# Turning the next chunk's sampling weights between the two samplings of a slot

## The chip, the cores and the metric

The kernel runs on one core of one Trainium2 chip. The metric is the device time of one execution in microseconds (us). The engines are TensorE (PE: matmuls and transposes), VectorE (DVE), ScalarE (ACT), GpSimd (POOL) and SyncE (SP, which only issues DMAs here). PE writes its results to PSUM, eight banks of 512 fp32 words in each of 128 partitions. The engines run in parallel, each through its own list of instructions in order, and meet only at semaphores.

## The reference

The input x has 4 images of 128 channels and 32 x 32 pixels. Cut to what matters:

```python
# L0, on the group-normalised x: a deformable 3x3 convolution
om = conv3x3(xn, w_off) + b_off              # 27 maps: 9 dy, 9 dx, 9 masks
for tap k, pixel p:                          # position p + tap + (dy, dx)
    sampled[k, p] = sigmoid(m) * bilinear(xn, at that position)
out = einsum('bckhw,ock->bohw', sampled, weight) + bias
x = x + groupnorm16(out) * gamma + beta
# L1, on the group-normalised x: two 3x3 convolutions with ternary weights
q1, q2 = ternary_quantize(w1), ternary_quantize(w2)
out1 = relu(batchnorm(conv3x3(xn, q1)))
x = x + relu(out1 + batchnorm(conv3x3(out1, q2)))
```

## The kernel before

Matmuls run in fp32r. To keep the accuracy each fp32 value is split in two: ACT copies the high part (names ending in hi), DVE subtracts it from the source (names ending in lo), and three matmuls take the place of one.

The deformable convolution is a loop over 36 chunks, 9 for each image (`CHUNKS`, `CH`). A chunk has two pairs of image rows, the last of an image (n % 9 == 8) has one. For a chunk GpSimd makes `vt` (L482): for each pixel and tap the weights of the 6 x 19 = 114 image pixels that bilinear sampling could reach. PE turns these weights by transposes into PSUM, with the 114 pixels on the partitions: eight taps of both pairs in 16 transposes (`turn_pairs_out`, L601, banks 0 and 1), or 6 in a chunk of one pair, and the last tap in one more (`turn_last_out`, L610, bank 2). ACT copies them to `shi` (L879 for the two pairs, L883 for the last tap), DVE makes `slo` (L1223, L1226). Then `sample(n, u)` (L629 to L631, six matmuls) multiplies the patch of pixels with these weights for pair u, into banks 3 and 4 or 5 and 6. ACT copies the result to `vhi` (L891), DVE makes `vlo` (L1234). At last `combine` (L647 to L649) multiplies two or three taps at a time with the layer's weights into bank 7, and ACT takes that out (L898).

The order is written out by hand: each engine has a function `slot(n)`, called for n = -2 to 35. In the kernel before, slot n holds

- on PE: sample pair 0 of chunk n; a piece of combining; sample pair 1 of chunk n; a wait for all three differences of chunk n+1 (`slo_ok` at 3n+6, L707); in some slots a small piece of other work (`beside`: sums for the normalisations L525 and L530, the ternary weights L659, L662, L670); the 16 transposes of chunk n+2; another piece of combining; the last tap's transpose of n+2
- on ACT: copy of pair 0's sampling; two steps of the hat functions of chunk n+4 (L870, L872); in every other slot the output of a finished row group (L898); in some slots the copy of ternary weights (L906); copy of pair 1's sampling; the copies of the weights of n+2 with the last tap's; other work
- on DVE: difference of pair 0; small reads of sums; difference of pair 1; the three differences of the weights of n+2; other work (statistics, ternary weights)
- on GpSimd, in a loop of its own: `vt`, which waits until the last tap's transpose two chunks back is done (L481)

Slots 10, 11, 19, 20, 28 and 29 lack a piece of combining. `shi` and `slo` have two halves, used by even and odd chunks. So the copies for chunk n+2 write the half that the samplings of chunk n read: `weights_hi(n + 2)` waits for `v_mm` of all pairs of chunk n (L877). A sampling increments `v_mm` when its last matmul is done. PSUM for the weights is there once: the transposes wait for the differences of the chunk before (L595, L609).

Behind the loop come the two ternary convolutions (L722) with their normalisations, and the stores.

Of the kernel before, what the change touches and what calls it, by code (L numbers as in the profile page):

```python
# [32 lines left out]
CHUNKS = B * CH  # L33
# [20 lines left out]
def build(nc, x, w_off, b_off, wd, bias, gamma, beta, w1, g1, be1, w2, g2, be2, out):  # L54
# [8 lines left out]
    with ExitStack() as ctx:  # L63
# [189 lines left out]
        def pairs(n):  # L253
            return 1 if n % CH == CH - 1 else 2
# [73 lines left out]
        def piece_at(n, place):  # L328

            m = 2 * n + place - 5  # L330
            b, r = m // (2 * CH), m % (2 * CH)
            return (b, r // 4, r % 4) if 0 <= b < B and r < 4 * WGRPS else None
# [172 lines left out]
        def _(pe):  # L505
# [85 lines left out]
            def turn_pairs_out(n):  # L591

                pe.wait_ge(vt_ok, n + 1)
                if n:
                    pe.wait_ge(slo_ok, 3 * n - 1)  # L595
                else:
                    pe.wait_ge(xtlo_ok, B)
                for tap in range(first_taps(n)):
                    for u in range(pairs(n)):
                        at = slice(u * P // 2, (u + 1) * P // 2)  # L600
                        ins = t.transpose(S_PAIR[u][:, tap, :], vt[at, n % 2, tap, :], ident[at, at])  # L601
                        if tap == first_taps(n) - 1:
                            ins.then_inc(s_mm, 1 if pairs(n) == 2 else 3)
# [94 lines left out]
            def slot(n):  # L698
                if n >= 0:
                    sample(n, 0)  # L700
                if piece_at(n, 0):
                    combine(*piece_at(n, 0))
                if n >= 0:
                    sample(n, 1)
                used = None
                if n >= 0 and n + 1 < CHUNKS:
                    pe.wait_ge(slo_ok, 3 * n + 6)  # L707
                    used = beside(n)
                if n + 2 < CHUNKS:
                    turn_pairs_out(n + 2)  # L710
                if piece_at(n, 1):
                    combine(*piece_at(n, 1))
                if n + 2 < CHUNKS:
                    if used:
                        pe.wait_ge(*used)
                    turn_last_out(n + 2)
# [45 lines left out]
            with pe.Else():  # L762
# [5 lines left out]
                n = SPECULATED - 1 + PATCHES  # L768
# [37 lines left out]
        def _(act):  # L806
# [67 lines left out]
            def weights_hi(n):  # L874
                act.wait_ge(s_mm, 3 * n + pairs(n) + (pairs(n) == 1) * 2)
                if n >= 2:
                    act.wait_ge(v_mm, pairs_through(n - 2))  # L877
                for u in range(pairs(n)):
                    a.activation(by_pair(shi, n)[:, u, 0:first_taps(n), :], S_PAIR[u][:, 0:first_taps(n), :],  # L879
                                 ACT.Copy).then_inc(shi_ok, 1 if pairs(n) == 2 else 3)  # L880
                if pairs(n) == 2:
                    act.wait_ge(s_mm, 3 * n + 3)
                    a.activation(by_pair(shi, n)[:, :, TAPS - 1, :], S_LAST.rearrange("k (u p) -> k u p", u=2),  # L883
                                 ACT.Copy).then_inc(shi_ok, 1)
# [19 lines left out]
            def copy_weights(i):  # L904
                act.wait_ge(q_t, i + 1)
                a.activation((q1, q2)[i // K][:, i % K * K:i % K * K + K, :],  # L906
                             Q_PS.rearrange("p (k o) -> p k o", k=K), ACT.Copy).then_inc(q_ok, 1)
# [18 lines left out]
            def slot(n):  # L926
                if n >= 0:
                    sampled_hi(n, 0)
                if n + 4 < CHUNKS:
                    hats(n + 4)  # L930
                if ends_in(n):
                    output(*ends_in(n))
                if n in TURNS:
                    copy_weights(TURNS.index(n))
                if n >= 0:
                    sampled_hi(n, 1)
                if n + 2 < CHUNKS:
                    weights_hi(n + 2)
                beside(n)

            def finish():
# [114 lines left out]
        def _(dve):  # L1056
# [162 lines left out]
            def weights_lo(n):  # L1219
                for u in range(pairs(n)):  # L1220
                    dve.wait_ge(shi_ok, 3 * n + (u + 1 if pairs(n) == 2 else 3))
                    src, hi, lo = (m[:, 0:first_taps(n), :] for m in (S_PAIR[u], by_pair(shi, n)[:, u, :, :], by_pair(slo, n)[:, u, :, :]))
                    d.tensor_tensor(lo, src, hi, ALU.subtract).then_inc(slo_ok, 1 if pairs(n) == 2 else 3)  # L1223
                if pairs(n) == 2:
                    dve.wait_ge(shi_ok, 3 * n + 3)
                    d.tensor_tensor(by_pair(slo, n)[:, :, TAPS - 1, :], S_LAST.rearrange("k (u p) -> k u p", u=2),  # L1226
                                    by_pair(shi, n)[:, :, TAPS - 1, :], ALU.subtract).then_inc(slo_ok, 1)
# [43 lines left out]
            def slot(n):  # L1271
                if n >= 0:
                    sampled_lo(n, 0)
                    sums_read(n)
                    sampled_lo(n, 1)
                if n + 2 < CHUNKS:
                    weights_lo(n + 2)
                beside(n)

            def finish():  # L1280
# [255 lines left out]
```

## Time and profile before

| | |
|---|---|
| median of 3 runs | 300.6 us (299.74 to 300.62) |
| the profiled execution | 300.69 us |
| its span, first to last instruction | 298.9 us |
| PE busy | 264.8 us, 89% |
| DVE busy | 203.4 us, 68% |
| ACT busy | 173.5 us, 58% |
| GpSimd busy | 133.0 us, 44% |
| mean granted clock of PE | 0.962 |

All durations below are of the one profiled execution. Times in rows count from the span's start. In a timeline each row is a run of like instructions: start, length, engine, line, operation, out<-in, shape, count; square brackets give the time for which the engine had stood idle before, and what ended that. Matmuls are pipelined: the end of one overlaps the start of the next, so the distance between two starts is the time that PE gives to a matmul, and its own length is longer.

### The profile page before, as it was taken

The page shows a single profiled execution, that of the slowest core. Times are in us where ns is not written, and L with a number is a line of the kernel's source. Part 1 is how long each engine was busy: PE and PEld are TensorE (multiplying, and loading weights), DVE is VectorE, ACT ScalarE, POOL GpSimd, SP SyncE. Part 2 cuts the span into 40 slices and gives each one's busy share as a digit, 9 for nine tenths or more (in the row PEclk, how much of TensorE's full clock was granted, in tenths as well). Part 3 has the DMA queues.
Part 4 walks back from the last instruction along what each step waited for, and adds up shares of the span by engine and source line. Part 5 has one row for each costly group of instructions (what it writes and reads, how often), then busy time and mean ns, then how long its engine had stood idle before and what let it go on. Part 6 is the DMA issues. An engine that isn't in the chain of part 4 may idle for free.

```text
span 298.9 us, 5513 instructions
## 1 busy us (share of the span) xinstructions
PE 264.8 (89%) x1956; PEld 230.6 (77%) x1956; DVE 203.4 (68%) x458; ACT 173.5 (58%) x366; POOL 133.0 (44%) x189
## 2 busy tenths in 40 slices
PE   2999999799989999998999989999899958999900
PEld 2778877689989789987998889998677737777700
DVE  4798668598988899659978699873374444115094
ACT  2449655588967987877799787871043015320051
POOL 8350276376866868787659976340000000000040
PEclk9999999899999999999999999999999996999965
DMA  7900867753433332333323333200000000000016
GB/s 245 337 19 3 259 194 232 247 153 133 136 124 117 108 113 75 106 107 115 107 80 108 113 122 114 67 0 2 0 0 0 2 0 1 0 0 2 2 37 250
DMA packets 25033, 28.63 MB, mean 96 GB/s; under 512 B 2461, under 2 KB 22541, under 8 KB 25000
## 3 DMA queue, kind: packets, MB, share of 16 engines
q1 hardware_dynamic: 24496, 26.98, 27.9%
q10 hardware_dynamic: 504, 1.24, 1.3%
q8 instruction: 18, 0.29, 0.4%
q14 instruction: 15, 0.12, 0.1%
HBM read 19.87 MB, written 6.78 MB: 89 GB/s over the span
## 4 chain that ended last, share of the span: by engine, by line
PE 75%; DVE 14%; ACT 7%; issue 2%; DMA 1%
PE PS L722 24%; PE PS L562 13%; PE PS L647 6%; PE PS L601 5%; PE PS L649 4%; PE PS L648 4%; PE PS L629 4%; PE PS L631 4%; PE PS L630 4%; DVE slo L1223 3%; ACT vhi L891 2%; DVE vlo L1234 2%; DVE xb L1326 2%; DVE st L1124 2%; DMA xs<-in_x 1%
## 5 line engine op out<-in xcount | busy, mean ns | idle before, releaser
L482 POOL TENSOR_TENSOR vt<-rowm,hat 128x1026 f32<-128x1026 f32 x36 | 70.8, 1966 | 30.3 <-PE PS L610 29.1
L1234 DVE TENSOR_TENSOR vlo<-PS,vhi 128x576 fp32r<-128x576 f32 (+2 forms) x88 | 50.0, 590 | 16.3 <-ACT vhi L891 15.8
L891 ACT ACTIVATE vhi<-PS 128x576 fp32r<-128x576 f32 (+2 forms) x88 | 43.8, 523 | 16.4 <-PE PS L631 16.2
L1223 DVE TENSOR_TENSOR slo<-PS,shi 114x512 fp32r<-114x512 f32 (+1 forms) x68 | 43.2, 673 | 3.3 <-ACT shi L879 3.0
L647 PE MATMUL PS<-vhi,wdhi 128*128 128x256 f32 x144 | 43.8, 304 | 1.8 <-ACT xb L898 1.8
L629 PE MATMUL PS<-shi,patch 114*128 114x288 f32 (+1 forms) x136 | 43.6, 320 | 2.0 <-DVE omh L1376 1.5
L722 PE MATMUL PS<-xhi,q 128*128 128x512 f32 (+1 forms) x144 | 39.2, 419 | 4.2 <-ACT xhi L958 4.2
L502 POOL TENSOR_TENSOR xb<-xb,xs 128x512 f32<-128x512 f32 x3 | 3.7, 1275 | 87.0 <-ACT xb L963 87.0
L631 PE MATMUL PS<-shi,patch 114*128 114x288 f32 (+1 forms) x136 | 40.8, 300 | 0.0
L630 PE MATMUL PS<-slo,patch 114*128 114x288 f32 (+1 forms) x136 | 40.7, 299 | 0.0
L648 PE MATMUL PS<-vlo,wdhi 128*128 128x256 f32 x144 | 40.6, 282 | 0.0
L649 PE MATMUL PS<-vhi,wdlo 128*128 128x256 f32 x144 | 40.5, 282 | 0.0
L879 ACT ACTIVATE shi<-PS 114x512 fp32r<-114x512 f32 (+1 forms) x68 | 36.7, 593 | 4.1 <-PE PS L601 3.5
L722 PE MATMUL PS<-xlo,q 128*128 128x512 f32 (+1 forms) x144 | 37.5, 405 | 0.0
L722 PEld LDWEIGHTS PS<-xhi,q 128*128 128x128 f32 x144 | 28.1, 198 | 11.7 <-ACT xhi L958 4.7
L722 PEld LDWEIGHTS PS<-xlo,q 128*128 128x128 f32 x144 | 27.5, 193 | 6.8
L647 PEld LDWEIGHTS PS<-vhi,wdhi 128*128 128x128 f32 x144 | 27.2, 189 | 4.0 <-issue 1.3
L629 PEld LDWEIGHTS PS<-shi,patch 114*128 114x128 f32 x136 | 26.5, 195 | 3.0 <-issue 2.8
L648 PEld LDWEIGHTS PS<-vlo,wdhi 128*128 128x128 f32 x144 | 27.3, 190 | 0.1
L649 PEld LDWEIGHTS PS<-vhi,wdlo 128*128 128x128 f32 x144 | 27.2, 189 | 0.0
L630 PEld LDWEIGHTS PS<-slo,patch 114*128 114x128 f32 x136 | 26.5, 195 | 0.0
L631 PEld LDWEIGHTS PS<-shi,patch 114*128 114x128 f32 x136 | 26.3, 193 | 0.0
(150 smaller groups left out, 464.3 us busy)
## 6 DMA issues: line engine op xcount, KB each, us to landing
patch<-xt SPq DMA_DIRECT2D x136, 114.0 KB
xt<-xtt SPq DMA_DIRECT2D x4, 1024.0 KB, 7.3
xs<-in_x SPq DMA_DIRECT2D x3, 512.0 KB, 7.3
out<-xb SPq DMA_DIRECT2D x6, 256.0 KB, 2.3
wraw<-in_L_conv_w SPq DMA_DIRECT2D x2, 576.0 KB, 9.2
omr<-omr SPq DMA_DIRECT2D x8, 128.0 KB, 3.9
wd_raw<-in_L_conv_weight ACTq DMA_DIRECT2D x1, 576.0 KB, 5.9
xs<-in_x SPq DMA_DIRECT2D x2, 256.0 KB, 4.1
```

What stands on the lines that cost most here:

```text
L482: g.tensor_tensor(vt[:, n % 2, :, :].rearrange("p t (r j) -> p t r j", r=WR), rowm[:, n % 2, :, :].unsqueeze(3).to_broadcast([P, TAPS, WR, ...
L562: last = t.matmul(tap_out(OFF_PS[(2 * b + h) % 4], h, k), woffT[:, k, :], tap_in((xhi, xlo)[part], b, h, k), start=(i == 0 and part == 0), ...
L629: t.matmul(v, patch[:, n % PATCHES, m, 0, :], hi[at], start=True, stop=False)
L630: t.matmul(v, patch[:, n % PATCHES, m, 0, :], lo[at], start=False, stop=False)
L631: last = t.matmul(v, patch[:, n % PATCHES, m, 1, :], hi[at], start=False, stop=True)
L647: t.matmul(O_PS, wdhi[:, w, :], hi, start=(tap == TAPS - 1), stop=False)
L648: t.matmul(O_PS, wdhi[:, w, :], lo, start=False, stop=False)
L649: last = t.matmul(O_PS, wdlo[:, w, :], hi, start=False, stop=(tap == 0))
L722: last = t.matmul(tap_out(PS[:, 2 * b + h, :], h, k), q[:, k, :], tap_in(src, b, h, k), start=(i == 0 and part == 0), stop=(i == TAPS - 1 ...
L891: last = a.activation(places(vhi), src, ACT.Copy)
L1223: d.tensor_tensor(lo, src, hi, ALU.subtract).then_inc(slo_ok, 1 if pairs(n) == 2 else 3)
L1234: last = d.tensor_tensor(places(vlo), src, places(vhi), ALU.subtract)
```

## The change

On all three engines the weights of the chunk two further on move between the two pairs' samplings. PE waits for chunk n+1's differences, does its small piece of other work and the 16 transposes ahead of the second sampling. ACT and DVE do the two pairs' copies and differences ahead of the second sampling's; the last tap's copy and difference are split off into functions of their own and follow the second sampling's. No instruction is added or taken away, and the waits keep their counts.

```diff
@@ -700,14 +700,14 @@
                     sample(n, 0)
                 if piece_at(n, 0):
                     combine(*piece_at(n, 0))
-                if n >= 0:
-                    sample(n, 1)
                 used = None
                 if n >= 0 and n + 1 < CHUNKS:
                     pe.wait_ge(slo_ok, 3 * n + 6)
                     used = beside(n)
                 if n + 2 < CHUNKS:
                     turn_pairs_out(n + 2)
+                if n >= 0:
+                    sample(n, 1)
                 if piece_at(n, 1):
                     combine(*piece_at(n, 1))
                 if n + 2 < CHUNKS:
@@ -878,6 +878,8 @@
                 for u in range(pairs(n)):
                     a.activation(by_pair(shi, n)[:, u, 0:first_taps(n), :], S_PAIR[u][:, 0:first_taps(n), :],
                                  ACT.Copy).then_inc(shi_ok, 1 if pairs(n) == 2 else 3)
+
+            def last_hi(n):
                 if pairs(n) == 2:
                     act.wait_ge(s_mm, 3 * n + 3)
                     a.activation(by_pair(shi, n)[:, :, TAPS - 1, :], S_LAST.rearrange("k (u p) -> k u p", u=2),
@@ -932,10 +934,12 @@
                     output(*ends_in(n))
                 if n in TURNS:
                     copy_weights(TURNS.index(n))
+                if n + 2 < CHUNKS:
+                    weights_hi(n + 2)
                 if n >= 0:
                     sampled_hi(n, 1)
                 if n + 2 < CHUNKS:
-                    weights_hi(n + 2)
+                    last_hi(n + 2)
                 beside(n)
 
             def finish():
@@ -1221,6 +1225,8 @@
                     dve.wait_ge(shi_ok, 3 * n + (u + 1 if pairs(n) == 2 else 3))
                     src, hi, lo = (m[:, 0:first_taps(n), :] for m in (S_PAIR[u], by_pair(shi, n)[:, u, :, :], by_pair(slo, n)[:, u, :, :]))
                     d.tensor_tensor(lo, src, hi, ALU.subtract).then_inc(slo_ok, 1 if pairs(n) == 2 else 3)
+
+            def last_lo(n):
                 if pairs(n) == 2:
                     dve.wait_ge(shi_ok, 3 * n + 3)
                     d.tensor_tensor(by_pair(slo, n)[:, :, TAPS - 1, :], S_LAST.rearrange("k (u p) -> k u p", u=2),
@@ -1272,9 +1278,12 @@
                 if n >= 0:
                     sampled_lo(n, 0)
                     sums_read(n)
+                if n + 2 < CHUNKS:
+                    weights_lo(n + 2)
+                if n >= 0:
                     sampled_lo(n, 1)
                 if n + 2 < CHUNKS:
-                    weights_lo(n + 2)
+                    last_lo(n + 2)
                 beside(n)
 
             def finish():
```

## Rows read from the trace of the kernel before

**Rows 1.** The page's 40 slices of the span: PE busy and granted clock, in tenths.

```profile
PE   2999999799989999998999989999899958999900
PEclk9999999899999999999999999999999996999965
```

**Rows 2.** PE's waits: line waited for, total us, times, longest.

```profile
PE PS L525 <- DVE mv L1132: 3.2, 4, 1.2
```

**Rows 3.** Timeline of PE, slots 3 to 5.

```profile
67.53 0.30 PE L629 MATMUL PS<-shi,patch 114*128 114x288 f32 x1
...
68.21 0.30 PE L631 MATMUL PS<-shi,patch 114*128 114x288 f32 x1
68.44 0.67 PE L601 MATMUL PS<-ident,vt 64*114 64x64 f32 x16
69.03 0.38 PE L647 MATMUL PS<-vhi,wdhi 128*128 128x256 f32 x1
...
69.88 0.38 PE L629 MATMUL PS<-shi,patch 114*128 114x288 f32 x1
...
71.49 0.31 PE L629 MATMUL PS<-shi,patch 114*128 114x288 f32 x1
...
75.81 0.30 PE L629 MATMUL PS<-shi,patch 114*128 114x288 f32 x1
```

**Rows 4.** Timelines of ACT and DVE, slot 3.

```profile
68.55 0.65 ACT L891 ACTIVATE vhi<-PS 128x576 fp32r<-128x576 f32 x1 [0.50 <-PE PS L631]
...
69.23 0.76 DVE L1234 TENSOR_TENSOR vlo<-PS,vhi 128x576 fp32r<-128x576 f32 x1 [1.09 <-ACT vhi L891]
69.90 1.28 DVE L1223 TENSOR_TENSOR slo<-PS,shi 114x512 fp32r<-114x512 f32 x2
71.10 0.28 DVE L1226 TENSOR_TENSOR slo<-PS,shi 114x128 fp32r<-114x128 f32 x1
```

**Rows 5.** Timelines of ACT and DVE, weights of slot 8, both engines free.

```profile
89.86 1.08 ACT L879 ACTIVATE shi<-PS 114x512 fp32r<-114x512 f32 x2 [0.99 <-PE PS L601]
...
90.49 1.29 DVE L1223 TENSOR_TENSOR slo<-PS,shi 114x512 fp32r<-114x512 f32 x2 [0.40 <-ACT shi L879]
```

**Rows 6.** Timelines of DVE and PE, slot 2, where PE waits.

```profile
63.79 0.28 DVE L1226 TENSOR_TENSOR slo<-PS,shi 114x128 fp32r<-114x128 f32 x1
...
64.13 0.67 PE L601 MATMUL PS<-ident,vt 64*114 64x64 f32 x16 [0.27 <-DVE slo L1226]
```

**Rows 7.** Timeline of PE: first and last of the loop's 34 transpose groups.

```profile
57.16 0.91 PE L601 MATMUL PS<-ident,vt 64*114 64x64 f32 x16
...
195.59 0.55 PE L601 MATMUL PS<-ident,vt 64*114 64x64 f32 x6
```

**Rows 8.** Timelines of DVE and PE, slots 18 and 19.

```profile
135.59 0.28 DVE L1226 TENSOR_TENSOR slo<-PS,shi 114x128 fp32r<-114x128 f32 x1
135.79 1.28 DVE L1124 BATCH_NORM_STATS2 st<-xs 128x6 f32<-128x512 f32 x2
...
137.74 0.44 PE L601 MATMUL PS<-ident,vt 64*114 64x64 f32 x8
```

**Rows 9.** Timeline of PE, slot 14.

```profile
114.94 0.50 PE L670 MATMUL PS<-ident,wraw 128*128 128x128 f32 x3
115.37 0.67 PE L601 MATMUL PS<-ident,vt 64*114 64x64 f32 x16
```

**Rows 10.** Timeline of PE, first samplings of slots 0 and 1.

```profile
55.50 0.33 PE L629 MATMUL PS<-shi,patch 114*128 114x192 f32 x1 [1.54 <-DVE omh L1376]
...
58.50 0.44 PE L630 MATMUL PS<-slo,patch 114*128 114x288 f32 x1
58.74 0.44 PE L631 MATMUL PS<-shi,patch 114*128 114x288 f32 x1
```

**Rows 11.** Stretches: length, busy time of PE, PEld, DVE, ACT, POOL, PEclk, DMA share, GB/s.

```profile
58.00:59.00 1.00, 1.00 (x7) 1.00 (x6) 0.58 (x1) 1.00 (x3) 0.65 (x2) 0.50 0.91 241
137.00:139.00 2.00, 1.54 (x23) 1.45 (x24) 1.92 (x7) 0.87 (x3) 0.41 (x3) 1.00 0.33 95
```

## The prediction

> **What bounds the kernel now.** I read the page's slices first. In [rows 1] the loop over the 36 chunks is slices 8 to 27 (each is 7.5 us): TensorE (PE) stands there at nines with some eights behind the first slice, and its granted clock (PEclk) is at the full level of 2.4 GHz but for that slice. The list of PE's waits comes next [rows 2]: the largest item of the loop is 3.2 us in all, at the group sums (L525). So the loop is bound by PE's own work, and a gain for another engine is worth nothing there, while a wait put on PE is paid in full. The order of time then gives the length of a slot [rows 3]. A sampling starts at 67.53, the next slot's at 71.49, the one after at 75.81: 3.96 us where the first combining of the next slot has two taps, 4.32 us where it has three. The weights' transposes start at 68.44, the combining behind them at 69.03: 0.60 us. A sampling takes 0.91 us of PE's time (67.53 to 68.44).
>
> The copies of the weights are off the path today, but by little. In [rows 4] ScalarE (ACT) takes the second sampling of slot 3 out at 68.55, VectorE (DVE) follows at 69.23, the two weight differences run from 69.90, the last tap's from 71.10 to 71.38. PE asks for them only after the second sampling of slot 4, at 71.49 + 0.91 = 72.40. So the cover is 1.02 us. The start of that sampling, 71.49, is 0.11 us after the copies' end; that is all that would be left if PE asked ahead of it and the copies kept their time.
>
> **The change, part by part.**
> (a) PE: the wait for chunk n+1's three differences, the sums beside, and the 16 transposes of chunk n+2 move ahead of the second sampling. The instructions are the same; each changeover between kinds of matmul occurs as often. Own cost: nothing. What it costs is cover: the wait comes 0.91 us earlier in its slot.
> (b) ACT: the two copies of the weights stand ahead of the second sampling's copy. They write the half of shi that chunk n's samplings read, so L877 keeps them waiting for v_mm of both pairs of chunk n. That is the end of the second sampling, which now stands behind the transposes. The copies can't start at the transposes' end, where the new order means them to: they start one sampling later. Queued behind that wait on ACT are only that sampling's own copy and the last tap's, which would wait for the same or later.
> (c) DVE: same order. The last tap's difference is now behind the second sampling's difference, and PE's wait before the transposes (slo_ok at 3n+6) counts all three differences, the last one too. So PE waits for the sampling's difference as well, without needing it.
>
> Together (a) to (c) close a ring: transposes of n+2, second sampling of n, copies, differences, last tap's difference, transposes of n+3. Its length from rows: transposes 0.60 [rows 3]; sampling from its start to the end of its last matmul, 67.53 to 68.21 + 0.30, 0.98, and 0.08 more right behind transposes, whose first matmul takes 0.38 instead of 0.30 (69.88), 1.06 [rows 3]; to ACT's start 0.04 (68.51 to 68.55); ACT's start to DVE's 0.63 (89.86 to 90.49 in [rows 5]); two differences 1.20 (69.90 to 71.10, [rows 4]); the sampling's difference 0.67 (69.23 to 69.90); the last tap's 0.28; to PE 0.06 (63.79 + 0.28 to 64.13, [rows 6]). Sum 4.54, say 4.55 us. ACT's own side, two copies and the sampling's, 1.08 + 0.65 = 1.73 [rows 4, 5], ends 0.1 us before DVE is through its pair (0.63 + 1.20), and hides.
>
> So each slot that has the ring lasts 4.55 us, instead of 3.96 or 4.32. The ring is in every slot n up to 32 that has a second pair (not 8, 17, 26) and doesn't prepare a chunk of one pair (not 6, 15, 24): 33 - 6 = 27 of the 33 steps. Between the first transposes of the loop at 57.16 and the last at 195.59 lie 138.43 us [rows 7]. After:
> - 27 x 4.55 = 122.9.
> - Steps whose wait is on a sum that DVE makes in its part beside the slot, behind the last tap's difference. The heaviest, slots 19 and 28 (two halves of statistics): last tap's difference done at 135.59 + 0.28, transposes at 137.74 [rows 8], 1.87, or 1.81 over the 0.06 counted already. The lighter, slots 8, 12, 21, 30, do half of that work or its like; the two halves take 1.28, so 1.81 - 0.64, 1.2. 2 x 1.81 + 4 x 1.2 = 8.4.
> - The turning of three ternary taps (L670) ahead of the transposes, 0.43 each time (114.94 to 115.37, [rows 9]), in four ring steps: 1.7. Six small matmul groups (slots 1, 13, 20, 22, 29, 31), between nothing and the 0.43 of the turns; I take 0.2: 1.2.
> - The 27th step is the first, on the low clock that is there before too (granted 0.50 in 58 to 59, [rows 11]): its PE part of 1.66 is longer; I add 0.6, an estimate between nothing and 1.66.
> - Six steps without the ring, by PE's own work: three at about 4.3 (as the 4.32 of [rows 3]), three a sampling shorter, 3.4 to 3.6: 23.5, an estimate.
> Sum 122.9 + 8.4 + 1.7 + 1.2 + 0.6 + 23.5 = 158.3, against 138.4: 19.9 us more. Both ends are moved by the same 0.91, so that is also the loop's growth. Behind the loop nothing new stands: the convolutions follow it on PE and start that much later. The profiled execution took 300.7 us with a span of 298.9, the median is 300.6; so 300.7 + 19.9 = 320.6.
>
> What moves off PE's wait is small. ACT and DVE get the ternary turns and group sums 0.91 us earlier in a slot, so their 1 to 2 us waits there shorten; they aren't the bound, and the ring takes their place. GpSimd (POOL) makes vt of a chunk as soon as the last tap's transpose two chunks back, at a slot's end, has freed its half, which is over a slot before PE asks for it; that transpose keeps its place, and PE asks a sampling earlier: nothing. SP's patch loads wait for v_mm of four chunks back: nothing.
>
> **The clock.** A wait of 1.54 us before 55.50 was followed by the low level of 1.2 GHz (a granted clock of 0.50 at 58 to 59, [rows 10, 11]); 0.46 us without work in 137 to 139 was not (1.00, [rows 11]). The new waits are 0.2 to 0.6 us in plain slots. But where a slot has few taps or a sum to wait for, PE's own work falls short of the ring by more: slot 10 to 11 has no combining, 0.60 + 2 x 0.91 + 0.1 = 2.5 of work in 4.55; 18 to 19, 4.0 in 6.4; 19 to 20, 2.7 in 4.85; likewise at 1, 7, 20 and 27 to 29. At five places waits of 1.5 to 2.3 us appear. A low stretch lengthens a ring step by 0.85 (the transposes 0.91 for 0.67, [rows 3, 7]; six matmuls 0.24 apart, 58.50 to 58.74 in [rows 10], for 0.68 / 5 = 0.14). Between 0 and about 7 of them (0 to 6 us); I take three, for the one wait of that size in the trace did it and shorter ones didn't: + 2.5. The forecast is 320.6 + 2.5 = 323.
>
> The Trainium skill, page "TensorE: Matmul & The Clock Gate", section "A second HAM failure mode: psum-queue depth-cycling", tells of a kernel in which short idle times between groups of matmuls alone made the clock go up and down. Of such short, regular waits the trace of before shows none, so it decides nothing yet; by that rule the time would be that of rival 1.
>
> **Rivals.**
> 1. The ring governs and the clock falls all through the loop, for PE then idles in nearly every slot. For it: the one low stretch followed a wait. Against: 137 to 139 kept 1.00 with 1.54 us busy in 2 [rows 11]. If half of 27 steps are low, 13.5 x 0.85 = 11.5: 332; if all, 344. Chance 0.12.
> 2. The ring is there but shorter than priced: a link is paid less (DVE finds its inputs ready, the end of a sampling is felt earlier than its modelled end). At 4.2 us the three-tap slots lose nothing and the two-tap ones 0.24: 27 x 0.35 = 9.5 less than 320.6, so 311. Against: each link is from a row. Chance 0.18.
> 3. PE stays the bound, the copies come in time everywhere. It needs a ring under 3.96, so 0.6 us less; the 0.11 us left in [rows 3, 4] would allow it only if the copies didn't start later, but L877 makes them. 300.6. Chance 0.04.
> 4. The other sign: PE's present waits at sums go, because they are asked for when DVE is further on. If all of L525 went [rows 2], 3.2 us: 297.5. It decides only if the ring is under 3.96 as well. But those sums come from DVE's part beside the slot before, and PE asks earlier. Chance 0.02.
> The change not doing what it says is part of the forecast: the copies stand between the samplings in the program, yet run after both.
>
> **How the numbers follow.** Forecast 323 with 0.64 (its own range 317 to 328: 0.1 us on the ring is 2.7 us, the clock 0 to 6). Rivals 0.12, 0.18, 0.04, 0.02. The range 309 to 334 takes in rival 2 and the lower half of rival 1 and leaves out under 0.15. A measurement of this kernel can tell about 0.3% from no change. Slower 0.94, same 0.04, faster 0.02.
>
> **What the profile after would show.** The step between transposes would be near 4.55 us in plain slots, both kinds alike. PE's largest wait in the loop would be at L601 for DVE slo L1226, some 10 us and over 15 times, or the same ended by the matmul before it. ACT's L879 would start 0.04 us after the last L631, not after L601, and DVE would run L1223 x2, L1234, L1226 in that order. PEclk would show single low slices near 65, 100, 145 and 185. Wrong if: L601 shows no wait (rival 3); L879 starts before the second sampling ends (my reading of L877 falls); the step is well under 4.4 (rival 2); PEclk is low in most slices (rival 1).

## The result, and the profile after

| | before | after |
|---|---|---|
| median | 300.6 us | 329.4 us |
| lowest to highest | 299.7 to 301.0 | 327.5 to 333.4 |
| ratio, 95% interval | | 1.094 [1.085, 1.104] |
| profiled execution, its span | 300.7, 298.9 | 327.5, 325.8 |
| first to last transposes of the loop | 138.4 [rows 7] | 163.6 |
| mean granted clock | 0.962 | 0.939 |

Slower by 28.8 us. Forecast were 323.0 in a range of 309 to 334. The executions of after are further apart than those of before; their granted clocks are too, 0.945 in one of 327.5 us and 0.925 in one of 331.3. The longest of the four executions of after (333.4 us, granted clock 0.914) was in a slower state and is left out of the ratio; the other three have a median of 327.5 us, 26.9 over before.

The page of after, its slices and its chain by engine, answers to [rows 1]; the chain of before stands behind it:

```profile
span 325.8 us, 5514 instructions
...
PE 271.7 (83%) x1956; PEld 236.4 (73%) x1956; DVE 200.7 (62%) x458; ACT 172.2 (53%) x366; POOL 133.2 (41%) x189
...
PE   2989998789989789995998978899989994999910
...
PEclk9998999969999999999799995999999997899975
...
PE 62%; DVE 24%; ACT 8%; DMA 2%; issue 2%; ACTq 0%
```

```profile
PE 75%; DVE 14%; ACT 7%; issue 2%; DMA 1%
```

The loop is slices 7 to 27 now (8.1 us each), and where PE stood at nines in most of them, with some eights, there are more eights, three sevens and a five (slice 18); PEclk has three low places (slices 8, 19 and 24, counted from 0). On the chain PE had 75% of the span and DVE 14%; now DVE has 24%. PE, DVE, ACT and POOL have as many instructions as before, so what was added is waiting, and a lower clock in three places.

PE's waits of after, and then the largest wait of DVE and of ACT (line, what it waited for, total us, times, longest; all over the whole execution). They answer to [rows 2]:

```profile
PE PS L525 <- DVE mv L1136: 9.3, 8, 2.1
PE PS L601 <- DVE slo L1232: 7.3, 10, 2.0
PE PS L530 <- DVE slo L1232: 5.2, 5, 2.0
...
PE PS L654 <- DVE slo L1232: 1.9, 1, 1.9
PE PS L670 <- DVE slo L1232: 1.7, 4, 0.7
```

```profile
DVE slo L1227 <- ACT shi L879: 45.2, 34, 3.2
ACT shi L879 <- PE PS L631: 44.5, 29, 3.3
```

L1232 is the last tap's difference (L1226 before). In before PE waited for it 1.2 us in all:

```profile
PE PS L530 <- DVE slo L1226: 0.6, 2, 0.3
...
PE PS L670 <- DVE slo L1226: 0.3, 1, 0.3
PE PS L601 <- DVE slo L1226: 0.3, 1, 0.3
```

Now it does so at four lines, 7.3 + 5.2 + 1.9 + 1.7 = 16.1 us, and the wait at the sums (L525) is 9.3 instead of 3.2. Of these, 6.3 and 1.4 lie in the loop. The fence on DVE and ACT is the ring from its other side: ACT's copy of the weights waits 29 times for the end of a sampling (L631), and DVE waits for ACT.

One turn of the ring, timelines of PE, ACT and DVE of after (start us, us, engine, line, count, idle before). They answer to [rows 3, 4]:

```profile
78.00 0.67 PE L601 MATMUL PS<-ident,vt 64*114 64x64 f32 x16 [0.57 <-DVE slo L1232]
78.60 0.40 PE L629 MATMUL PS<-shi,patch 114*128 114x288 f32 x1
...
79.39 0.30 PE L631 MATMUL PS<-shi,patch 114*128 114x288 f32 x1
...
82.62 0.67 PE L601 MATMUL PS<-ident,vt 64*114 64x64 f32 x16 [0.24 <-DVE slo L1232]
```

```profile
79.78 1.09 ACT L879 ACTIVATE shi<-PS 114x512 fp32r<-114x512 f32 x2 [1.03 <-PE PS L631]
80.75 0.66 ACT L893 ACTIVATE vhi<-PS 128x576 fp32r<-128x576 f32 x1
```

```profile
80.41 1.29 DVE L1227 TENSOR_TENSOR slo<-PS,shi 114x512 fp32r<-114x512 f32 x2 [0.35 <-ACT shi L879]
81.62 0.75 DVE L1240 TENSOR_TENSOR vlo<-PS,vhi 128x576 fp32r<-128x576 f32 x1
82.28 0.28 DVE L1232 TENSOR_TENSOR slo<-PS,shi 114x128 fp32r<-114x128 f32 x1
```

Read it as a sum: transposes 0.60, sampling from 78.60 to 79.39 + 0.30, 1.09; ACT starts 0.09 behind that; DVE 0.63 behind ACT; two differences 1.21; the sampling's 0.66; the last tap's 0.28; PE 0.06 behind it. 0.60 + 1.09 + 0.09 + 0.63 + 1.21 + 0.66 + 0.28 + 0.06 = 4.62, and the next transposes do start at 82.62. ACT had been idle for 1.03 us when it began at 79.78, with its input ready since the transposes' end at 78.67: the wait at L877 for the second sampling held it, as step (b) of the prediction has it.

### The profile page after: what moved, and what is told of

The parts are those of the page before. It is cut to its first block, busy times and chain, and to the rows that moved or that the text cites. A ratio compares the mean times of both kernels' runs of the same rounds, so it can differ in the third digit from the quotient of the medians.

```text
span 325.8 us, 5514 instructions
## 1 busy us (share of the span) xinstructions
PE 271.7 (83%) x1956; PEld 236.4 (73%) x1956; DVE 200.7 (62%) x458; ACT 172.2 (53%) x366; POOL 133.2 (41%) x189
## 4 chain that ended last, share of the span: by engine, by line
PE 62%; DVE 24%; ACT 8%; DMA 2%; issue 2%; ACTq 0%
PE PS L722 22%; DVE slo L1227 9%; PE PS L562 9%; PE PS L601 7%; PE PS L629 5%; ACT shi L879 5%; DVE vlo L1240 4%; PE PS L631 4%; PE PS L630 3%; PE PS L647 2%; DMA wd_raw<-in_L_conv_weight 2%; DVE st L1128 2%; PE PS L648 2%; PE PS L649 2%; DVE xb L1335 2%
## 5 line engine op out<-in xcount | busy, mean ns | idle before, releaser
L482 POOL TENSOR_TENSOR vt<-rowm,hat 128x1026 f32<-128x1026 f32 x36 | 70.7, 1964 | 49.3 <-PE PS L610 48.3
L1227 DVE TENSOR_TENSOR slo<-PS,shi 114x512 fp32r<-114x512 f32 (+1 forms) x68 | 43.4, 677 | 45.2 <-ACT shi L879 45.2
L879 ACT ACTIVATE shi<-PS 114x512 fp32r<-114x512 f32 (+1 forms) x68 | 36.7, 589 | 46.1 <-PE PS L631 44.5
L629 PE MATMUL PS<-shi,patch 114*128 114x288 f32 (+1 forms) x136 | 47.5, 350 | 1.5 <-DVE omh L1385 1.5
L893 ACT ACTIVATE vhi<-PS 128x576 fp32r<-128x576 f32 (+2 forms) x88 | 44.8, 542 | 3.8 <-PE PS L631 3.7
L647 PE MATMUL PS<-vhi,wdhi 128*128 128x256 f32 x144 | 41.9, 291 | 1.0 <-ACT xb L900 1.0
L631 PE MATMUL PS<-shi,patch 114*128 114x288 f32 (+1 forms) x136 | 42.1, 309 | 0.0
L630 PE MATMUL PS<-slo,patch 114*128 114x288 f32 (+1 forms) x136 | 41.9, 308 | 0.0
L722 PEld LDWEIGHTS PS<-xhi,q 128*128 128x128 f32 x144 | 28.2, 199 | 11.6 <-ACT xhi L962 4.7
L601 PE MATMUL PS<-ident,vt 64*114 64x64 f32 x536 | 24.4, 229 | 7.4 <-DVE slo L1232 7.3
L629 PEld LDWEIGHTS PS<-shi,patch 114*128 114x128 f32 x136 | 27.0, 198 | 4.3 <-issue 2.0
L647 PEld LDWEIGHTS PS<-vhi,wdhi 128*128 128x128 f32 x144 | 28.0, 195 | 1.7 <-DVE vlo L1240 0.8
L601 PEld LDWEIGHTS PS<-ident,vt 64*114 64x114 f32 x536 | 19.4, 137 | 12.1 <-DVE slo L1232 9.8
L648 PEld LDWEIGHTS PS<-vlo,wdhi 128*128 128x128 f32 x144 | 28.0, 195 | 0.1
```

Source lines behind the costliest of these rows:

```text
L482: g.tensor_tensor(vt[:, n % 2, :, :].rearrange("p t (r j) -> p t r j", r=WR), rowm[:, n % 2, :, :].unsqueeze(3).to_broadcast([P, TAPS, WR, ...
L629: t.matmul(v, patch[:, n % PATCHES, m, 0, :], hi[at], start=True, stop=False)
L630: t.matmul(v, patch[:, n % PATCHES, m, 0, :], lo[at], start=False, stop=False)
L631: last = t.matmul(v, patch[:, n % PATCHES, m, 1, :], hi[at], start=False, stop=True)
L647: t.matmul(O_PS, wdhi[:, w, :], hi, start=(tap == TAPS - 1), stop=False)
L648: t.matmul(O_PS, wdhi[:, w, :], lo, start=False, stop=False)
```

## Where the 25 us of the loop are

Step by step, from one group of L601 to the next, the profiled execution of after compares with the terms of the forecast like this. The nine steps that have the ring and nothing else took 4.61 to 4.63 us.

| term | forecast | measured |
|---|---|---|
| 27 ring steps | 27 x 4.55 = 122.9 | 27 x 4.61 = 124.5 |
| sums in the wait | 8.4 | heavy 1.83 + 1.81, light 0.64, 1.23, 1.2, 1.2: 7.9 |
| turns (L670) | 1.7 | 4 x 0.55 = 2.2 |
| six small groups | 1.2 | 5 x 0.31, and 0.12 (L654): 1.7 |
| low clock of the first step | 0.6 | 0 |
| six steps without ring | 23.5 | 4.10, 3.67, 4.45, 3.70, 4.68, 3.36: 24.0 |
| low clock elsewhere | 2.5 | 0.27, 1.16, 0.52, 0.19, 1.18: 3.3 |
| loop | 160.8 | 163.6 |

For slots 20 to 21 and 29 to 30 (6.33 and 7.00) the light sum and the low clock fall together; I split them by the 1.23 that the same sum costs at slot 11 to 12. The loop grew by 163.6 - 138.4 = 25.2 us, the span by 26.9. The rest is start-up: the transposes ahead of the loop began 1.7 us later than before (50.43 against 48.70). That is no effect of the change: in the kernels below these transposes begin between 48.62 (pair 0 not waiting, the new order on PE) and 51.06 (the last kernel, the old order), early or late in either order.

The granted clock in stretches of after (window, length, busy of PE, PEld, DVE, ACT and POOL, PEclk, DMA share, GB/s), to set beside [rows 11]:

```profile
60.00:65.00 5.00, 3.06 (x32) 2.69 (x31) 3.04 (x7) 3.01 (x8) 2.92 (x4) 0.90 0.68 195
65.00:70.00 5.00, 3.72 (x27) 3.25 (x27) 2.81 (x5) 2.78 (x7) 2.92 (x4) 0.50 0.37 127
...
78.00:88.00 10.00, 9.19 (x93) 8.58 (x94) 9.11 (x16) 8.61 (x19) 6.57 (x12) 1.00 0.28 86
...
105.00:110.00 5.00, 2.99 (x45) 2.68 (x43) 3.01 (x6) 3.78 (x9) 3.43 (x6) 1.00 0.33 102
...
155.00:160.00 5.00, 5.00 (x39) 4.92 (x40) 2.52 (x6) 1.91 (x5) 1.24 (x2) 0.66 0.31 88
```

In 78 to 88 PE waits 0.57, 0.24 and 0.57 us, and its clock stays at the full level; the low level of 1.2 GHz stands in 65 to 70, behind PE busy for 3.06 us of 60 to 65 with a wait of 1.94, and in part of 155 to 160 and of 195 to 205, behind waits of 1.5 to 2.1 us. Not each such wait did it: one of 2.01 ended at 109.47, and the clock stayed at 1.00 in 105 to 110 and behind it to 120. The section "A second HAM failure mode: psum-queue depth-cycling" of the Trainium skill's page "TensorE: Matmul & The Clock Gate" would have the clock go up and down with short idle times between groups alone. Here the regular ones of 0.2 to 0.6 us in plain steps of 4.6 us didn't do it (1.00 in 78 to 88): the trace doesn't bear the rule out for this kernel.

## The experiments

The theory: the time is the ring of step (a) to (c), three links of which the new order made: PE asks a sampling earlier, ACT waits at L877 for a sampling that now stands behind the transposes, and PE's wait counts a difference that stands behind the second sampling's. Its rivals: DVE or ACT are themselves made slower by their new order; PE's clock; the waits of the sums. The first has the page against it: DVE was busy for 200.7 us, in before for 203.4, and ACT for 172.2 against 173.5.

**PE's part alone.** The kernel before, with only the change's first piece:

```diff
                     combine(*piece_at(n, 0))
-                if n >= 0:
-                    sample(n, 1)
                 used = None
@@
                     turn_pairs_out(n + 2)
+                if n >= 0:
+                    sample(n, 1)
```

> The kernel before with the new order on PE alone; ACT and DVE keep theirs (second sampling's copy first, then the weights). Theory (a ring through PE's wait at 3n+6): the ring is 0.60 + 1.06 + 0.04 to ACT, 0.68 to DVE, then the sampling's difference 0.67, two weight differences 1.21, the last tap's 0.28 and 0.06 to PE, 4.60 us, as long as after the whole change; so 325 to 330 us and plain steps of 4.6. Rival (the new order of the copies is what costs): near the kernel before, 300 to 303.

Measured: 326.6 us, 1.089 [1.082, 1.095] of before, in the expected range. Plain steps of 4.59 to 4.62, the loop 161.6. The ring needs no more than PE's move: DVE's and ACT's old order, with the sampling's copy ahead of the weights', makes the same circle, for both copies wait for the same sampling and the sum of the links is one sum in either order.

**ACT's and DVE's part alone.** The kernel after, with PE's piece undone:

```diff
                     combine(*piece_at(n, 0))
+                if n >= 0:
+                    sample(n, 1)
                 used = None
@@
                     turn_pairs_out(n + 2)
-                if n >= 0:
-                    sample(n, 1)
```

> The kernel before with the new order on ACT and DVE alone; PE samples both pairs before it transposes, as before. Theory: from the transposes' start the last tap's difference is done after 0.74 + 0.63 + 1.21 + 0.67 + 0.28 + 0.06 = 3.6 us, under the 3.97 of a plain slot, so plain steps stay at 3.97 and 4.31; only steps with no combining (3.1 to 3.2 now) grow to 3.6, and the six steps with a DVE sum by 0.65 each: 302 to 307 us. Rival (the order of the copies costs by itself): 325 to 330.

Measured: 318.3 us, 1.057 [1.050, 1.065]. A miss for the theory and for its rivals: plain steps take 4.45 us. PE's waits and a turn of it:

```profile
PE PS L629 <- DVE vlo L1240: 11.2, 16, 1.7
```

```profile
76.66 0.67 PE L601 MATMUL PS<-ident,vt 64*114 64x64 f32 x16
...
80.12 0.38 PE L629 MATMUL PS<-shi,patch 114*128 114x288 f32 x1
...
81.11 0.67 PE L601 MATMUL PS<-ident,vt 64*114 64x64 f32 x16
```

```profile
77.39 1.09 ACT L879 ACTIVATE shi<-PS 114x512 fp32r<-114x512 f32 x2 [0.75 <-PE PS L601]
```

```profile
78.03 1.29 DVE L1227 TENSOR_TENSOR slo<-PS,shi 114x512 fp32r<-114x512 f32 x2 [0.18 <-ACT shi L879]
79.23 0.75 DVE L1240 TENSOR_TENSOR vlo<-PS,vhi 128x576 fp32r<-128x576 f32 x1
```

There is a second ring. The second sampling of chunk n+1 writes the banks 5 and 6 from which DVE makes vlo of the second sampling of chunk n, and vlo now stands behind the weights' differences. From the transposes at 76.66: 0.73 to ACT, 0.64 to DVE, 1.20 for two differences, 0.75 for vlo, 0.14 to the sampling that waited, at 80.12, and 0.99 for it up to the transposes at 81.11: 4.45. So the moved order on ACT and DVE costs 17 us of its own; with PE's order too, the first ring is the longer one and hides this one.

**The third link: the last tap's difference first.** The kernel after, with this on ACT and likewise on DVE:

```diff
                     weights_hi(n + 2)
-                if n >= 0:
-                    sampled_hi(n, 1)
                 if n + 2 < CHUNKS:
                     last_hi(n + 2)
+                if n >= 0:
+                    sampled_hi(n, 1)
```

> The changed kernel, but on ACT and DVE the last tap's copy and difference stand ahead of the second sampling's. Theory: the second sampling's difference (0.67) leaves the ring, 4.61 becomes 3.94; slots with three taps in front go back to PE's own 4.31, two-tap slots to 3.97, the slots with sums and without combining lose 0.67: some 27 x 0.5 = 14 us less, 311 to 315 us, less again if low clock stretches go with the waits. Rival (the extra time is the clock, not the ring): the low stretches stay where sums are waited for, at most 3 us change.

Measured: 318.2 us, 1.055 [1.048, 1.061], above the expected range. Plain steps are back at 3.95 to 3.98, or 4.34 with three taps, as the link of 0.67 says. But the steps with sums stay as long as in after or get longer (6.62 at 18 to 19, 6.43 at 27 to 28, 7.14 and 7.16 at 20 to 21 and 29 to 30; in after 6.44, 6.42, 6.33 and 7.00), since the sums still stand behind the sampling's difference:

```profile
143.13 0.56 PE L525 MATMUL PS<-mv,g 128*128 128x1 f32 x2 [2.10 <-DVE mv L1136]
143.62 0.68 PE L601 MATMUL PS<-ident,vt 64*114 64x64 f32 x8
```

The expectation had these steps lose 0.67 each. Three steps without a sum also got longer, 0.3 to 0.7 us each (4.89, 4.72 and 5.36 at 4 to 5, 6 to 7 and 24 to 25).

**The second link: pair 0 need not wait for the second sampling.** The kernel after, where the copy of pair 0's weights waits for pair 0's sampling alone:

```diff
-                if n >= 2:
-                    act.wait_ge(v_mm, pairs_through(n - 2))
                 for u in range(pairs(n)):
+                    if n >= 2:
+                        act.wait_ge(v_mm, min(pair_no(n - 2, u) + 1, pairs_through(n - 2)))
```

> The changed kernel, but the copy of pair 0's weights waits only for pair 0's sampling of chunk n, pair 1's copy for pair 1's: each half of the buffer half has its own wait. Theory (the copies start at the end of the second sampling because of this wait): one difference of 0.6 leaves the ring, 4.61 becomes about 4.0: 311 to 315 us, L879's first copy starts behind L601 and the second 0.04 behind the last L631. Rival (the copies start late for another cause, the transposes or ACT's own queue): no change, 327.

Measured: 311.3 us, 1.034 [1.029, 1.039], in the expected range and 16 to 18 us less than after, by the median without or with its longest execution. This wait alone takes 14.3 us out of the loop (149.3 for 163.6). Plain steps are 3.97 and 4.31, as of before. The copy of pair 0 starts at the end of the transposes (70.74) where pair 1's still waits for the end of the sampling (71.75), so one copy less lies behind the sampling:

```profile
70.80 0.60 ACT L879 ACTIVATE shi<-PS 114x512 fp32r<-114x512 f32 x1 [0.28 <-PE PS L601]
71.79 0.60 ACT L879 ACTIVATE shi<-PS 114x512 fp32r<-114x512 f32 x1 [0.38 <-PE PS L631]
```

Steps with sums keep up to 6.3 (5.76, 5.94, 5.77, 6.33).

**PE's wait on all three differences, only where something needs the third.** The kernel after, where PE waits for all three ahead of the transposes only in the slots that do side work there; in the others the transposes wait for the first two. `has_beside(n)`, not shown, says which: 19 slots, not the 20 of the expectation.

```diff
                 if n >= 0 and n + 1 < CHUNKS:
-                    pe.wait_ge(slo_ok, 3 * n + 6)
+                    if has_beside(n):
+                        pe.wait_ge(slo_ok, 3 * n + 6)
                     used = beside(n)
```

> The changed kernel, but PE waits for all three differences of chunk n+1 only in the 20 slots in which it writes sums or ternary weights into the last tap's bank; in the others the transposes' own wait for the two pairs' differences is left. Theory: without the sampling's difference and the last tap's the ring is 4.61 - 0.67 - 0.21 = 3.7, so steps into plain slots fall to PE's own 3.97 and 4.31 while steps into the 20 others stay as after the change; about ten plain steps x 0.5 and two without combining: 320 to 323 us. Rival (it is the copies' late start alone that PE feels, not which difference it waits for): 327.

Measured: 326.4 us, 1.080 [1.072, 1.087]: a miss. The interval overlaps after's, so a gain isn't shown. Eight steps did fall from 4.61 to between 3.84 and 3.98, or to 4.34, which is 5.0 us together. They were given back in others. Steps behind a shortened one are longer than in after (4.90, 4.70, 5.34 for 4.62, 4.10, 4.68). That would follow if the copies' chain didn't get faster, which isn't shown. The clock is low more often: 6.43 us at slot 2 to 3, where after has 5.77, and over 55 to 225 us it was 0.92 granted, in after 0.95. The loop is 163.0 us, after's 163.6. Whether the clock fell by chance of this execution isn't shown.

**The side work behind the second sampling.** The kernel after, with the wait for three and the side work moved behind the second sampling, so that the transposes wait for two differences only:

```diff
                 used = None
-                if n >= 0 and n + 1 < CHUNKS:
-                    pe.wait_ge(slo_ok, 3 * n + 6)
-                    used = beside(n)
                 if n + 2 < CHUNKS:
                     turn_pairs_out(n + 2)
                 if n >= 0:
                     sample(n, 1)
+                if n >= 0 and n + 1 < CHUNKS:
+                    pe.wait_ge(slo_ok, 3 * n + 6)
+                    used = beside(n)
```

> The changed kernel, but the wait for all three differences and the small work beside the slot come behind the second sampling; only the transposes, with their own wait, stand between the samplings. Theory: the ring through the transposes is 3.7 us and PE's wait at the sums has a sampling more of cover; plain steps 3.97 and 4.31, steps without combining 3.7, sum steps as in the kernel before or shorter: 300 to 303 us. Rival (transposes between the samplings cost by themselves, by the second ring through the banks of the second sampling or by the changeovers): 305 or more.

Measured: 313.1 us, 1.042 [1.038, 1.047]: 16 us less than after, yet 10 more than expected; the rival on record, with 305 or more, did better. The loop is 147.6. Plain steps are at 3.97 at 3 to 4, 5 to 6 and 32 to 33, but 4.90, 5.10 and 4.50 at 4 to 5, 9 to 10 and 23 to 24; the heavy sums at 4.49 and 3.98 (6.44 and 6.42 in after): with PE's question for the sums put off, that term is gone. What is left are other waits: 3.0 us at the transposes for the pairs' differences (L601 for L1227), 2.2 at samplings for vlo (1.6 of it at once), 1.9 at the last tap's transpose, and a single step of 6.40 at slot 15 to 16. That one step, 2 us over its 4.43 of before, holds the wait of 1.6; its cause stands below, under the side work alone. How much the second ring adds isn't shown.

**Both.** The same kernel with the pair-0 wait of above.

```diff
+                    if n >= 2:
+                        act.wait_ge(v_mm, min(pair_no(n - 2, u) + 1, pairs_through(n - 2)))
```

> The one before it, and pair 0's copy of the weights waits only for pair 0's sampling. Theory: the ring shortens once more, by 0.6 to 3.1, which matters only in the steps without combining: 298 to 301 us.

Measured: 306.4 us, 1.020 [1.016, 1.023]: a miss. The wait at L877 is worth 6.7 us here by the medians and 4.6 in the loop (143.0), but the kernel is still 5.5 us slower than before; the step at slot 15 to 16 is 6.37.

**The side work alone, in the order of before.** The kernel before, the wait for three and the side work behind the transposes:

```diff
                 used = None
+                if n + 2 < CHUNKS:
+                    turn_pairs_out(n + 2)
                 if n >= 0 and n + 1 < CHUNKS:
                     pe.wait_ge(slo_ok, 3 * n + 6)
                     used = beside(n)
-                if n + 2 < CHUNKS:
-                    turn_pairs_out(n + 2)
```

> The kernel before with one edit on PE: the wait for all three differences and the small work beside the slot come behind the transposes instead of ahead of them. Theory: PE's waits for DVE's sums (3.2 us in all at L525, 0.9 at L659) get 0.6 us more cover in each of some seven places; the reads of the sums come later on DVE by as much, off the path: 298 to 300 us. Rival (the waits only move to the last tap's transpose, which waits for what follows the sum): no change, 300.9.

Measured: 309.2 us, 1.030 [1.025, 1.034]: a miss, on the wrong side of before. The loop is 146.7, 8.3 more than before, and three steps hold that: 7.99 at slot 15 to 16, 7.06 at 24 to 25 and 5.80 at 19 to 20 (4.43, 4.87 and 3.22 in before). The first one's timelines of DVE and POOL:

```profile
120.23 0.16 DVE L1115 SCALAR_TENSOR_TENSOR nsm<-nsm 128x1 f32<-128x1 f32 x1
...
120.42 1.95 DVE L1119 SCALAR_TENSOR_TENSOR nsm<-nsm,vec 128x1 f32<-128x1 f32 x1
...
122.29 1.41 DVE L1234 TENSOR_TENSOR vlo<-PS,vhi 128x576 fp32r<-128x576 f32 x2
```

```profile
120.40 1.96 POOL L482 TENSOR_TENSOR vt<-rowm,hat 128x1026 f32<-128x1026 f32 x1
```

```profile
123.18 0.58 PE L629 MATMUL PS<-shi,patch 114*128 114x288 f32 x1 [1.82 <-DVE vlo L1234]
```

A DVE instruction of one element in each partition lasted 1.95 us, and ended with GpSimd's L482 beside it. In the kernel before it took 0.33, at another place against GpSimd's work (timelines of DVE and POOL):

```profile
119.54 0.33 DVE L1119 SCALAR_TENSOR_TENSOR nsm<-nsm,vec 128x1 f32<-128x1 f32 x1
```

```profile
119.37 0.49 POOL L466 TENSOR_TENSOR hat<-omr,ctab 128x171 f32<-128x171 f32 x1
```

There it began beside GpSimd's short L466 and ended with that, at 119.87 against 119.86. In the changed kernel it met the long one. Where nothing of GpSimd runs beside it, as at 195.67 in before, it takes 0.22. The side work behind the second sampling (two sections above) met the long one too, in its step of 6.40 (L1123 is the same instruction):

```profile
125.61 1.95 DVE L1123 SCALAR_TENSOR_TENSOR nsm<-nsm,vec 128x1 f32<-128x1 f32 x1
```

```profile
125.58 1.96 POOL L482 TENSOR_TENSOR vt<-rowm,hat 128x1026 f32<-128x1026 f32 x1
```

So did the version with both edits, for 1.93 us in its step of 6.37.

What stands behind it on DVE came late, PE waited 1.82 us, and the clock was 0.54 in 123 to 125. So to ask for the sums later wasn't free here: it put a small normalisation step into another place against GpSimd. That explains the first of the three steps only. At slot 24 to 25 the same instruction took 0.22, and PE waited 1.45 us for vlo at L647; the causes there and at 19 to 20 are open.

**Adding a known cost.** The main step of the argument is that DVE's time in the chain is covered in before and paid in full in after. So pair 1's difference is made twice in either kernel, 0.72 us more of DVE for each chunk of two pairs (`again` is a semaphore of its own, its making not shown):

```diff
+                    if u == 1:
+                        d.tensor_tensor(lo, src, hi, ALU.subtract).then_inc(again, 1)
+                        dve.wait_ge(again, sum(pairs(m) == 2 for m in range(n + 1)))
                     d.tensor_tensor(lo, src, hi, ALU.subtract).then_inc(slo_ok, 1 if pairs(n) == 2 else 3)
```

In the kernel before:

> The kernel before with one difference doubled: DVE computes pair 1's weight difference twice, one after the other, about 0.75 us more in each of the 31 chunks of two pairs that it is paid for. Theory: plain slots have 1.02 us of cover and hide it; it is paid where there is none: four steps without combining (0.7 each), some 3 us in the steps that wait for a DVE sum, and where DVE's own work fills the slot (eight slots with 1.3 us of work beside): 306 to 312 us in all. Rival (a microsecond of DVE work costs the same wherever it stands): as much as in the changed kernel.

Measured: 312.1 us, 1.038 [1.035, 1.042]. In the kernel after:

> The changed kernel with the same difference doubled. Theory: it lies in the ring, so each of the 27 ring steps grows by the whole 0.75 us, 4.61 to 5.35: 20 us more than the changed kernel, 345 to 351 us. Rival (PE's waits have slack that can take it, or the clock is what was paid for): under 10 us more, 337 or less.

Measured: 351.0 us, 1.168 [1.164, 1.172]. Two transposes of after with the addition (its lines are one further down):

```profile
77.20 0.67 PE L602 MATMUL PS<-ident,vt 64*114 64x64 f32 x16 [0.50 <-DVE slo L1236]
82.53 0.67 PE L602 MATMUL PS<-ident,vt 64*114 64x64 f32 x16 [1.30 <-DVE slo L1236]
```

Both times are at the upper end of what was expected. A plain step is 5.33 us, 4.61 + 0.72: each added hundredth is paid. The loop went from 163.6 to 187.1 (58.85 to 245.94), 23.5 us, of which 27 x 0.72 = 19.4 are the ring and the rest sums and clock. In before the loop grew by 11.6 us, half as much. Ten of the 33 steps stayed within 0.02 us, among them the plain ones at 2 to 3, 3 to 4, 31 to 32 and 32 to 33 (4.32, 3.96, 4.34 and 3.96): there the addition was covered. It is paid where DVE also works on ternary weights or statistics (steps of 4.5 to 5.9 us), in steps without combining (3.63 for 2.91 and 3.08), and in one step on the low clock (6.25 for 4.44). The cover of the kernel before is there, but plain slots alone tell too much of it.

**The order of before, with less to wait for.** What is left of PE's waits in the loop of before are small ones, the sums' (L525) the largest with 1.4 us. Three small pieces are moved there: the first half of an image's statistics a slot earlier, a sign change of the ternary weights' extremes one slot earlier, and ACT's output of a row group ahead of the hat functions in slots 24 and 26. PE waits for all three differences only in the slots with side work. The diff shows the first piece only:

```diff
+                        if n == CH * (b + 2) - 1:
+                            dve.wait_ge(x1_ok, 2 * b + 1)
+                            half_stats(GN1, b, 0)
                         if n == CH * (b + 2):
-                            stats_x1(b)
+                            dve.wait_ge(x1_ok, 2 * b + 2)
+                            image_stats(GN1, b, halves=(1,))
```

> The kernel before in its old order with PE's remaining waits in the loop attacked: the first half of the statistics for slots 19 and 28 one slot earlier, the sign change of the ternary extremes one slot earlier, the output ahead of the hat functions in slots 24 and 26, and the wait for all three differences only in the 20 slots that need it. Theory: the waits before slots 8, 19 and 28 shrink by 0.6, 0.6 and 0.5, those in slots 24 and 26 by 0.7 and 0.3, in slots 2 and 11 by 0.2 each: 3 us less than the kernel before, 297 to 299 us. Rival (each wait removed comes back at the next one): 300.5 to 301.5.

Measured: 298.4 us, 0.992 [0.989, 0.994] of before: 2.4 us less, in the expected range. That is clear of noise, but under the 2% from which a time is called faster here. The loop is 135.4 against 138.4. One of the waits that shrink is this one of slot 19, here 0.27, in before 0.89 (the step 4.60 for 5.19):

```profile
138.08 0.35 PE L525 MATMUL PS<-mv,g 128*128 128x1 f32 x2 [0.27 <-DVE mv L1141]
```

The four pieces stand in one kernel, so what each brings isn't shown.

## Why the prediction was right

**What bounds the kernel.** Right in the main. In before PE's work is the bound, and in slot 3 the copies have 1.02 us of cover: the twice-made difference didn't lengthen the plain steps of before at 2 to 4 and 31 to 33, and lengthened those of after by all of itself. Two readings went too far. The 1.02 us don't hold in every slot, for half of the addition was paid in before. And the 3.2 us at L525 [rows 2] are of the whole execution, 1.4 of them in the loop; rival 4's 297.5 rested on all 3.2.

**(a) PE's move.** Right, and more than the text said: PE's part alone costs 25.7 us, and 23.2 of the loop's 25.2. "Own cost: nothing" holds: the instructions are as many, and the cost is cover that is gone, with the low clock behind some of the waits. What it was to show did show: L601 waits for the last tap's difference, 7.3 us in 10 waits rather than some 10 in over 15; where a small group or a turn comes first, the same wait stands at L530, L654 and L670.

**(b) ACT.** Right. L879 starts 0.09 us behind the end of the last L631 and not behind L601, and where pair 0 is freed of that wait, plain steps are PE's own again (311.3 us). The prediction didn't ask what the moved copies do without PE's move: they make the second ring through banks 5 and 6, which sets the step (4.45) when PE's move is undone; after's own is longer.

**(c) DVE.** Right in mechanism: with the last tap's difference ahead, plain steps are 3.97. Wrong in that "together (a) to (c) close a ring" sounds as if all three were needed; PE's move is enough.

**The ring's price.** 4.55 forecast, 4.61 measured. The link from the sampling's modelled end to ACT was taken as 0.04; it was 0.09. Why isn't shown: with pair 0 freed, pair 1's copy starts 0.04 behind it again. The sampling behind transposes took 1.09 for 1.06 (the first matmul 0.40). 27 x 0.06 = 1.6 us.

**Sums and small pieces.** The heavy sums were forecast at 1.81 from [rows 8] and measured 1.82. Turns cost 0.55 for 0.43, past the bound that I had set. Five of the six small groups cost 0.31 and one 0.12, for the 0.2 that I took. Both terms together: 0.5 + 0.5 us. The first of the light sums cost half of what I took (0.5 us less), and the loop's first step was on the full clock here, 4.61 without its small group (its transposes 0.67, not the 0.91 of [rows 7]), 0.6 less than forecast.

**The clock.** Three low stretches forecast and three found, of 3.3 us for 2.5. That the number fits is partly luck: three was picked between 0 and 7, of the places named (near 65, 100, 145, 185) only the first was right, the others were at 156 and 200, and what sorts the waits that are followed by a low clock from those that aren't stays open. Rival 1 falls: in plain slots the clock stays full.

**Time.** 2.8 of the loop, 1.7 of start-up and 1.9 between the profiled execution and the median make the 6.4 us from 323.0 to 329.4. Of these, only the loop's terms belong to the working. The start-up differs from execution to execution and happened to be late here. The 1.9 is the longest execution's doing: the median of the other three is 327.5, that of the profiled one. The loop's terms missed by up to 1.6 us, and 1.1 us too much (light sums, first step) offset part of 3.9 too little.

**Rivals.** 2 would have needed a ring of 4.2, it was 4.61; 3 and 4 needed it under 3.96. The kernel with pair 0 freed comes out at rival 2's time, 311.3, but by another way: its plain steps are PE's own 3.97 and 4.31, not 4.2, and its sums cost more.

## What to carry to other kernels

When a consumer is put ahead of other work in an in-order engine, two things are to be read first: how long before the end of its cover its inputs are ready, and what else on the same buffers now stands between them. A move that adds no instruction can close a ring through buffers that exist once or twice, and the ring's length is the sum of links that each trace row gives; here it was right to 0.06 us in 4.6. A wait on a count also waits for everything counted: a wait for only what is needed (pair 0 alone) gave back 14.3 of the loop's 25.2 us. And to find where a chain has cover, add a known cost to it in both kernels, and read the slots apart: the cover read in one plain slot didn't hold in most of the others.

## What the runs showed of the hardware

The DVE instruction L1119, 128 x 1, took 0.22 us alone and 1.95 beside a GpSimd instruction (L482, 128 x 1026, 1.96 us), with which it ended; three kernels show it, with 1.95, 1.95 and 1.93. It reads two tensors in SBUF. The Trainium skill, page "SBUF — State Buffer", section "SBUF: two separate sides", says that VectorE and GpSimd share one pair of ports, that an instruction of VectorE with two inputs in SBUF needs it against a GpSimd instruction that reads SBUF, and that whichever starts first holds it for its whole instruction while the other blocks. The rows agree: L482 began at 120.40, L1119 at 120.42, and they ended at 122.36 and 122.37, though L1119 handles one element in each partition.

Second, the regular waits of 0.2 to 0.6 us in plain steps of 4.6 us left TensorE's clock at 2.4 GHz in after (1.00 in 78 to 88), and so did those of 0.5 to 1.3 us in steps of 5.33 us with the twice-made difference (1.00 in 77 to 88, PE busy 8.54 us of 11). The low level of 1.2 GHz came behind longer ones (0.50 in 65 to 70, behind one of 1.94), but not behind each (1.00 in 105 to 110, with one of 2.01).
